# The sums of two layer norms: bf16 copies and bf16 squares replaced by float32 operands

## The chip, the cores and the metric

The kernel runs on all 8 cores of one Trainium2 chip. The metric is the device time in microseconds of the slowest core. The median of 3 runs is 2408.73 us (2408.63 to 2413.28).

## The reference

One transformer layer, with a layer norm behind each of its two parts, over x of shape (2, 4096, 2048) in float32:

```python
x = layernorm(x + attention(x, Wq, Wk, Wv, Wo))   # 16 query heads, 4 KV heads, window 512
x = layernorm(x + ffn(x, ...))                    # silu(x Wg') * (x Wu'), then Wd'; 2048 -> 8192 -> 2048
# layernorm: (x - mean) / sqrt(var + 1e-5) over the last axis (2048), with no scale and no bias
# Wg, Wu, Wd are integers 0..255: (w - 128) * a scale for each output row
```

## The kernel before

Each core computes 1024 tokens (and reads 512 more for the keys and values of its window). Activations lie transposed: the 2048 features are 16 blocks (KC = 16) of 128 partitions, the tokens lie along the free axis. The residual stream is S_sb, float32, 128 x (16 x 1024). All else that is large lies in one bf16 tile, ab, cut by offsets (abv(offset, n)).

The stages follow one another: projections for v, q and k; attention; the output projection psW (L465), whose results VectorE adds to S_sb (L474); the first layer norm; the feed-forward in two halves of 32 blocks (gate psG L685, up psU L693, then the sums of h psH L751 for the zero point, then the down projection psD, which starts each output with two float32 matmuls of one row, L791, and goes on with L795), whose results VectorE adds to S_sb (L805); the second layer norm; the output. Instructions are written engine by engine, and semaphores (tm for TensorE, vv for VectorE, ss for ScalarE, and others for DMA) order them. barrier() makes every engine wait for all counts so far; there is one before and one at the end of each norm. The first weights of the feed-forward are requested by GpSimd after the first norm's barrier.

emit_ln writes a layer norm. The features lie on partitions, so a sum over them is a matmul with a column of ones: out is 1 x 512. Its steps, with their lines:

1. ScalarE copies S_sb to bf16, 16 copies of 128 x 1024 (L499, to abv(rbf_o)).
2. First sum: for each half of the tokens (tt) 16 matmuls over k, ones_cb (bf16) against the copies, into psS1 (L511). Those of tt = 0 wait each for their copy.
3. ScalarE squares S_sb, 32 pieces of 128 x 512, to one of two bf16 buffers (L527); each waits until the matmul two before has read its buffer.
4. Second sum: 32 matmuls of the ones against the squares, into psS2 (L537), each of which waits for its square. Two float32 matmuls of 1 x 1 against 1 x 512 add eps (L542).
5. Mean, variance, reciprocal and root on one partition, by VectorE and ScalarE in turn (L551 to L580), then four float32 matmuls (L586 to L589) which spread both rows over 128 partitions.
6. VectorE multiplies and subtracts, 16 instructions each (L600, L605). In the first norm ScalarE writes the bf16 copy y1 of the result (L612).

Both norms call it with the copies' place free for them: y1_o in the first, h_o in the second. sq_sb is a float32 tile of 128 x 1024, in use in the feed-forward (L720 writes it) and for the mean in the norm. onc_sb is a float32 column of ones that is loaded at the start, and oncb_sb the bf16 one.

Of the kernel before, what the change touches and what calls it, by code (L numbers as in the profile page):

```python
# [19 lines left out]
KC = D // 128  # L20
# [8 lines left out]
def build_nc(debug=False, upto=99, dumps=None):  # L29
# [33 lines left out]
    with contextlib.ExitStack() as ctx:  # L63
        S_sb = ctx.enter_context(nc.sbuf_tensor("S_sb", [128, KC * T], F32))
        ab = ctx.enter_context(nc.sbuf_tensor("ab", [128, 65536], BF16))
        sq_sb = ctx.enter_context(nc.sbuf_tensor("sq_sb", [128, 1024], F32))
# [3 lines left out]
        onc_sb = ctx.enter_context(nc.sbuf_tensor("onc_sb", [128, 1], F32))  # L70
# [4 lines left out]
        oncb_sb = ctx.enter_context(nc.sbuf_tensor("oncb_sb", [128, 1], BF16))  # L75
        eps_sb = ctx.enter_context(nc.sbuf_tensor("eps_sb", [1, 512], F32))

        def abv(off, n):
            return ab[:, off:off + n]
# [9 lines left out]
        ss = ctx.enter_context(nc.semaphore("ss"))  # L89
# [7 lines left out]
        cnt = {k: 0 for k in sems}  # L97

        def inc(instr, name, step=1):
            cnt[name] += step  # L100
            instr.then_inc(sems[name], step)
            return cnt[name]
# [5 lines left out]
        block = ctx.enter_context(nc.Block())  # L108
# [377 lines left out]
        def emit_ln(write_bf16_to=None, rbf_o=None):  # L486
            _ln_id[0] += 1
            li = _ln_id[0]
            with nc.psum_tensor(f"psS1_{li}", [1, 1024], F32) as psS1, \
                 nc.psum_tensor(f"psS2_{li}", [1, 1024], F32) as psS2, \  # L490
                 nc.psum_tensor(f"psB1_{li}", [128, 1024], F32) as psB1, \
                 nc.psum_tensor(f"psB2_{li}", [128, 1024], F32) as psB2:
                ss0_rc = cnt["ss"]
                c_rc = [ss0_rc + k + 1 for k in range(KC)]

                @block.scalar
                def _(s):
                    for k in range(KC):
                        got = inc(s.copy(abv(rbf_o + 1024 * k, 1024),  # L499
                                         S_sb[:, 1024 * k:1024 * k + 1024]), "ss")  # L500
                        assert got == c_rc[k]

                @block.tensor
                def _(t):
                    t.wait_ge(sq, p0_sq)
                    last = None
                    for tt in range(2):
                        for k in range(KC):
                            if tt == 0:
                                t.wait_ge(ss, c_rc[k])  # L510
                            last = t.matmul(psS1[:1, 512 * tt:512 * tt + 512], oncb_sb[:, :1],  # L511
                                            abv(rbf_o + 1024 * k + 512 * tt, 512),
                                            start=(k == 0), stop=(k == KC - 1))
                    inc(last, "tm")
                tm0_sq = cnt["tm"]
                c_smm = [tm0_sq + j + 1 for j in range(2 * KC)]
                ss0_sq = cnt["ss"]
                c_sq = [ss0_sq + j + 1 for j in range(2 * KC)]

                @block.scalar  # L520
                def _(s):
                    for j in range(2 * KC):
                        tt, k = j // KC, j % KC
                        if j >= 2:
                            s.wait_ge(tm, c_smm[j - 2])
                        got = inc(
                            s.activation(abv(rbf_o + 16384 + 512 * (j % 2), 512),  # L527
                                         S_sb[:, 1024 * k + 512 * tt:1024 * k + 512 * tt + 512],
                                         AF.Square), "ss")
                        assert got == c_sq[j]  # L530

                @block.tensor
                def _(t):
                    for j in range(2 * KC):
                        tt, k = j // KC, j % KC
                        t.wait_ge(ss, c_sq[j])
                        got = t.matmul(psS2[:1, 512 * tt:512 * tt + 512], oncb_sb[:, :1],  # L537
                                       abv(rbf_o + 16384 + 512 * (j % 2), 512),
                                       start=(k == 0), stop=False)
                        assert inc(got, "tm") == c_smm[j]  # L540
                    for tt in range(2):
                        inc(t.matmul(psS2[:1, 512 * tt:512 * tt + 512], onr_sb[:1, :1],  # L542
                                     eps_sb[:1, :], start=False, stop=True), "tm")
                tm_sums = cnt["tm"]

                psM = sq_sb[0:1, 0:1024]
                psQ2 = st_sb[:1, 0:1024]
                @block.vector
                def _(v):
                    v.wait_ge(tm, tm_sums)  # L550
                    inc(v.tensor_scalar(psM, psS1[:1, :], 1.0 / D, None, ALU.mult), "vv")  # L551
                c1 = cnt["vv"]

                @block.scalar
                def _(s):
                    s.wait_ge(vv, c1)
                    inc(s.activation(psQ2, psM, AF.Square), "ss")
                c2 = cnt["ss"]

                @block.vector  # L560
                def _(v):
                    v.wait_ge(ss, c2)
                    inc(v.scalar_tensor_tensor(psS2[:1, :], psS2[:1, :], 1.0 / D,
                                               psQ2, ALU.mult, ALU.subtract), "vv")
                    v.wait_ge(vv, cnt["vv"])
                    inc(v.reciprocal(psS2[:1, :], psS2[:1, :]), "vv")
                c3 = cnt["vv"]

                @block.scalar
                def _(s):  # L570
                    s.wait_ge(vv, c3)
                    inc(s.activation(psS2[:1, :], psS2[:1, :], AF.Sqrt), "ss")
                c4 = cnt["ss"]

                @block.vector
                def _(v):
                    v.wait_ge(ss, c4)
                    inc(v.tensor_tensor(psQ2, psM, psS2[:1, :], ALU.mult), "vv")
                    v.wait_ge(vv, cnt["vv"])
                    inc(v.tensor_copy(psM, psS2[:1, :]), "vv")  # L580
                c5 = cnt["vv"]

                @block.tensor
                def _(t):
                    t.wait_ge(vv, c5)
                    t.matmul(psB1[:, 0:512], onr_sb[:1, :], sq_sb[0:1, 0:512], start=True, stop=True)  # L586
                    t.matmul(psB1[:, 512:1024], onr_sb[:1, :], sq_sb[0:1, 512:1024], start=True, stop=True)
                    t.matmul(psB2[:, 0:512], onr_sb[:1, :], st_sb[:1, 0:512], start=True, stop=True)
                    inc(t.matmul(psB2[:, 512:1024], onr_sb[:1, :], st_sb[:1, 512:1024],  # L589
                                 start=True, stop=True), "tm")  # L590
                tm_bc = cnt["tm"]

                ln_done = [None] * KC

                @block.vector
                def _(v, ln_done=ln_done):
                    v.wait_ge(tm, tm_bc)
                    for k in range(KC):
                        sl = S_sb[:, 1024 * k:1024 * k + 1024]
                        inc(v.tensor_tensor(sl, sl, psB1[:, :], ALU.mult), "vv")  # L600
                    mid = cnt["vv"]
                    v.wait_ge(vv, mid)
                    for k in range(KC):
                        sl = S_sb[:, 1024 * k:1024 * k + 1024]
                        ln_done[k] = inc(v.tensor_tensor(sl, sl, psB2[:, :], ALU.subtract), "vv")  # L605

                if write_bf16_to is not None:
                    @block.scalar
                    def _(s, ln_done=ln_done):
                        for k in range(KC):  # L610
                            s.wait_ge(vv, ln_done[k])
                            inc(s.copy(abv(write_bf16_to + 1024 * k, 1024),  # L612
                                       S_sb[:, 1024 * k:1024 * k + 1024]), "ss")

                barrier()
                return ln_done

        emit_ln(write_bf16_to=y1_o, rbf_o=y1_o)

        if debug and "y1" in dumps:  # L620
# [198 lines left out]
        if debug and "r2" in dumps:  # L819
# [4 lines left out]
            barrier()  # L824

        ln2_done = emit_ln(write_bf16_to=None, rbf_o=h_o)

        @block.sync
# [93 lines left out]
```

## Time and profile before

| what | us |
|---|---|
| median of 3 runs | 2408.73 |
| the profiled execution: its time | 2411.91 |
| its span on the slowest core (core 4) | 2410.3 |
| spans of the 8 cores | 2394.1 to 2410.3 |
| first norm, from the table load to the end of y1 | 711.14 to 820.61 |
| second norm, its first record | 2277.82 |

The profile is that of core 4, and every time of the rows below is counted from the start of its span. PE is TensorE's matmuls, PEld its weight loads, DVE is VectorE, ACT ScalarE, POOL GpSimd. The granted clock of TensorE is given as a share of 2.4 GHz: 1.00 is 2.4, 0.50 is 1.2 GHz. TensorE is busy 83% of the span, VectorE 20%, ScalarE 15%, and the mean granted clock is 0.901.

### The profile page before, as it was taken

The page shows a single profiled execution, that of the slowest core. Times are in us where ns is not written, and L with a number is a line of the kernel's source. Part 1 is how long each engine was busy: PE and PEld are TensorE (multiplying, and loading weights), DVE is VectorE, ACT ScalarE, POOL GpSimd, SP SyncE. Part 2 cuts the span into 40 slices and gives each one's busy share as a digit, 9 for nine tenths or more (in the row PEclk, how much of TensorE's full clock was granted, in tenths as well). Part 3 has the DMA queues.
Part 4 walks back from the last instruction along what each step waited for, and adds up shares of the span by engine and source line. Part 5 has one row for each costly group of instructions (what it writes and reads, how often), then busy time and mean ns, then how long its engine had stood idle before and what let it go on. Part 6 is the DMA issues. An engine that isn't in the chain of part 4 may idle for free.

```text
span 2410.3 us, 23828 instructions; the slowest of 8 cores (2394.1 to 2410.3 us)
## 1 busy us (share of the span) xinstructions
PE 2012.4 (83%) x9317; PEld 916.8 (38%) x9496; DVE 471.0 (20%) x800; ACT 367.0 (15%) x640; POOL 129.0 (5%) x248
## 2 busy tenths in 40 slices
PE   0789766666985299999999999999999999999850
PEld 0334344444431144444443444444444443444310
DVE  0111266665111510010010000010010010000025
ACT  0000055555014301001010000001001010000140
POOL 4000000000000000000000000000000000000000
PEclk9999966666995599999999999999999999999955
DMA  9444200000430354344333333344344330333103
GB/s 218 62 92 70 53 1 1 1 1 1 70 53 0 53 89 87 70 75 83 70 71 53 70 64 58 67 74 87 70 75 83 70 71 18 70 65 58 35 0 139
DMA packets 38419, 147.68 MB, mean 61 GB/s; under 512 B 4643, under 2 KB 8869, under 8 KB 33958
## 3 DMA queue, kind: packets, MB, share of 16 engines
q0 software_dynamic: 35136, 127.94, 30.2%
q1 hardware_dynamic: 3174, 18.20, 2.3%
q8 instruction: 79, 1.29, 0.2%
q14 instruction: 30, 0.25, 0.0%
HBM read 265.66 MB, written 8.39 MB: 114 GB/s over the span
## 4 chain that ended last, share of the span: by engine, by line
PE 78%; DVE 7%; issue 4%; ACT 4%; another core or an unknown queue 3%; DMA 2%; DVEq 0%; ACTq 0%; POOL 0%; POOLq 0%
PE psD L795 19%; PE psG L685 18%; PE psU L693 18%; PE psW L465 5%; PE psQ L218 5%; PE psD L791 3%; PE pT L345 3%; PE pv L358 2%; DVE S_sb L600 2%; DVE S_sb L605 1%; PE psH L751 1%; ACT ab L499 1%; PE psQ L227 1%; DVE Dm_sb L386 1%
## 5 line engine op out<-in xcount | busy, mean ns | idle before, releaser
L685 PE MATMUL psG<-ab 128*128 128x512 bf16 x2006 | 451.5, 380 | 51.4 <-DMA ab<-wu_is 47.2
L795 PE MATMUL psD<-ab 128*128 128x512 bf16 x2004 | 449.9, 381 | 4.8 <-issue 3.7
L693 PE MATMUL psU<-ab 128*128 128x512 bf16 x2008 | 450.0, 379 | 2.1
L685 PEld LDWEIGHTS psG<-ab 128*128 128x128 bf16 x2048 | 200.7, 98 | 293.8 <-issue 54.1
L795 PEld LDWEIGHTS psD<-ab 128*128 128x128 bf16 x2048 | 195.8, 98 | 277.7 <-issue 52.9
L693 PEld LDWEIGHTS psU<-ab 128*128 128x128 bf16 x2048 | 200.2, 98 | 241.8
L705 DVE SCALAR_TENSOR_TENSOR ab<-psU,scl_sb,sq_sb 128x512 bf16<-128x512 f32 x128 | 90.2, 746 | 810.3 <-PE psU L693 810.3
L720 ACT ACTIVATE sq_sb<-psG,scl_sb 128x512 f32<-128x512 f32 x128 | 87.9, 687 | 775.1 <-PE psG L685 775.1
L345 PE MATMUL pT<-Dm_sb,ab 128*128 128x128 bf16 x640 | 77.4, 274 | 100.5 <-DVE Dm_sb L386 60.3
L805 DVE SCALAR_TENSOR_TENSOR S_sb<-psD,scl_sb,S_sb 128x1024 f32<-128x1024 f32 x32 | 41.1, 1283 | 481.5 <-PE psD L795 481.5
L218 PE MATMUL psQ<-ab 128*128 128x512 bf16 x501 | 111.6, 383 | 12.6 <-DMA ab<-wq_os 11.9
L465 PE MATMUL psW<-ab 128*128 128x512 bf16 x502 | 112.4, 385 | 1.3 <-DVE ab L378 0.8
L345 PEld LDWEIGHTS pT<-Dm_sb,ab 128*128 128x128 bf16 x640 | 50.9, 119 | 161.7 <-issue 161.7
L400 ACT ACTIVATE ab<-sc 128x640 bf16<-128x640 f32 x128 | 90.0, 703 | 118.3 <-DVE sc L372 107.6
L372 DVE TENSOR_TENSOR sc<-sc,ab 128x640 f32<-128x640 f32 x128 | 105.5, 825 | 1.8 <-PE sc L336 0.9
L407 ACT CAST ab<-pT 128x640 bf16<-128x640 f32 x128 | 87.5, 684 | 2.8 <-PE pT L345 2.8
L183 PE MATMUL psA<-ab 128*128 128x512 bf16 x95 | 23.9, 407 | 74.5 <-DMA ab<-x_all 74.5
L358 PE MATMUL pv<-ab 128*128 128x128 bf16 x640 | 84.8, 289 | 0.5 <-DVE ab L378 0.5
L106 POOL DMA_DIRECT2D ab<-wg_is x64 | 33.8, 527 | 915.6 <-PE psU L693 726.2
L218 PEld LDWEIGHTS psQ<-ab 128*128 128x128 bf16 x512 | 50.4, 99 | 73.8 <-issue 14.6
L465 PEld LDWEIGHTS psW<-ab 128*128 128x128 bf16 x512 | 50.5, 99 | 63.0 <-issue 4.1
L791 PE MATMUL psD<-st_sb,nr_sb 1*128 1x512 f32 x128 | 71.9, 641 | 2.9 <-DVE st_sb L760 2.9
(74 smaller groups left out, 935.7 us busy)
## 6 DMA issues: line engine op xcount, KB each, us to landing
ab<-wg_is POOLq DMA_DIRECT2D x64, 512.0 KB, 5.0
ab<-wu_is POOLq DMA_DIRECT2D x64, 512.0 KB, 7.0
ab<-wd_os POOLq DMA_DIRECT2D x32, 1024.0 KB, 8.0
ab<-wq_os POOLq DMA_DIRECT2D x16, 512.0 KB, 5.0
ab<-wo_os POOLq DMA_DIRECT2D x16, 512.0 KB, 5.0
y<-S_sb SPq DMA_DIRECT2D x16, 512.0 KB, 6.7
ab<-x_all POOLq DMA_DIRECT2D x16, 256.0 KB, 45.6
ab<-wv_ks POOLq DMA_DIRECT2D x16, 128.0 KB, 32.1
```

Of the source, the lines that this page charges most:

```text
L218: last = t.matmul(ps[:, 512 * tt:512 * tt + 512], abv(wbuf_o + 2048 * (o % 2) + 128 * k, 128), abv(rhs_base + k * rhs_stride + rhs_off + 5 ...
L345: last = t.matmul(pTp[:, 128 * b:128 * b + 128], abv(probs_o + 640 * (m % 3) + 128 * b, 128), Dm_sb[:, 128 * (m % 3):128 * (m % 3) + 128], ...
L358: last = t.matmul(pvs[m % 2][:, :], abv(vT_o + 512 * (mqt + b) + 128 * (mh // 4), 128), abv(pT_o + 640 * (m % 2) + 128 * b, 128), start=(b ...
L372: assert inc(v.tensor_tensor(scs[n % 2][:, :], scs[n % 2][:, :], abv(mask_o + 640 * qt, 640), ALU.add), "vv") == c_msk[n]
L400: s.activation(abv(probs_o + 640 * (n % 3), 640), scs[n % 2][:, :], AF.Exp, bias=0.0, scale=1.0 / 128.0, accum_out=sums_sb[:, 2 * (n % 3): ...
L465: last = t.matmul(psQ[o % 2][:, 512 * tt:512 * tt + 512], abv(wbuf_o + 2048 * (o % 2) + 128 * k, 128), abv(attn_o + 1024 * k + 512 * tt, 512),
L685: last = t.matmul(psG[i % 2][:, 512 * tt:512 * tt + 512], abv(wgu_o + 4096 * (i % 2) + 128 * k, 128), abv(y1_o + 1024 * k + 512 * tt, 512) ...
L693: last = t.matmul(psU[i % 2][:, 512 * tt:512 * tt + 512], abv(wgu_o + 4096 * (i % 2) + 2048 + 128 * k, 128), abv(y1_o + 1024 * k + 512 * t ...
L705: v.scalar_tensor_tensor(abv(h_o + 1024 * i + 512 * tt, 512), psU[i % 2][:, 512 * tt:512 * tt + 512], scl_sb[:, 64 + ii:64 + ii + 1], sq_s ...
L720: s.activation(sq_sb[:, 512 * tt:512 * tt + 512], psG[i % 2][:, 512 * tt:512 * tt + 512], AF.Silu, bias=0.0, scale=scl_sb[:, ii:ii + 1]), ...
L791: t.matmul(psD[o % 2][:, 512 * tt:512 * tt + 512], nr_sb[:1, :], st_sb[:1, 512 * tt:512 * tt + 512], start=True, stop=False)
L795: last = t.matmul(psD[o % 2][:, 512 * tt:512 * tt + 512], abv(wd_o + 4096 * (o % 2) + 128 * i, 128), abv(h_o + 1024 * i + 512 * tt, 512), ...
```

## The change

In emit_ln the 16 copies to bf16 go, with the waits for them. The matmuls of the first sum read S_sb itself, in float32, with the float32 ones. The squares are written as float32 to the two halves of sq_sb, and the matmuls of the second sum read these with the float32 ones. Counts, order and buffering of the squares and of all that follows stay. The function is called twice.

```diff
-                ss0_rc = cnt["ss"]
-                c_rc = [ss0_rc + k + 1 for k in range(KC)]
-
-                @block.scalar
-                def _(s):
-                    for k in range(KC):
-                        got = inc(s.copy(abv(rbf_o + 1024 * k, 1024),
-                                         S_sb[:, 1024 * k:1024 * k + 1024]), "ss")
-                        assert got == c_rc[k]
-
                 @block.tensor
                 def _(t):
                     t.wait_ge(sq, p0_sq)
                     last = None
                     for tt in range(2):
                         for k in range(KC):
-                            if tt == 0:
-                                t.wait_ge(ss, c_rc[k])
-                            last = t.matmul(psS1[:1, 512 * tt:512 * tt + 512], oncb_sb[:, :1],
-                                            abv(rbf_o + 1024 * k + 512 * tt, 512),
+                            last = t.matmul(psS1[:1, 512 * tt:512 * tt + 512], onc_sb[:, :1],
+                                            S_sb[:, 1024 * k + 512 * tt:1024 * k + 512 * tt + 512],
                                             start=(k == 0), stop=(k == KC - 1))
                     inc(last, "tm")
...
                         got = inc(
-                            s.activation(abv(rbf_o + 16384 + 512 * (j % 2), 512),
+                            s.activation(sq_sb[:, 512 * (j % 2):512 * (j % 2) + 512],
                                          S_sb[:, 1024 * k + 512 * tt:1024 * k + 512 * tt + 512],
                                          AF.Square), "ss")
...
                         t.wait_ge(ss, c_sq[j])
-                        got = t.matmul(psS2[:1, 512 * tt:512 * tt + 512], oncb_sb[:, :1],
-                                       abv(rbf_o + 16384 + 512 * (j % 2), 512),
+                        got = t.matmul(psS2[:1, 512 * tt:512 * tt + 512], onc_sb[:, :1],
+                                       sq_sb[:, 512 * (j % 2):512 * (j % 2) + 512],
                                        start=(k == 0), stop=False)
```

## Rows read from the trace of the kernel before

**Rows 1.** Busy time by stretch, two stretches of the first norm's sums, with the columns' names.

```profile
core 4: us, PE busy (x) PEld busy (x) DVE busy (x) ACT busy (x) POOL busy (x), PEclk, DMA share, GB/s
...
711.00:729.00 18.00, 9.71 (x18) 1.55 (x19) 0.00 (x0) 17.82 (x19) 0.00 (x0) 0.58 0.00 0
729.00:757.00 28.00, 21.70 (x50) 4.07 (x49) 0.00 (x0) 18.36 (x32) 0.00 (x0) 0.62 0.00 0
```

**Rows 2.** The timeline of the first norm: start, length, engine, line, instruction [idle before].

```profile
709.62 1.22 DVE L474 TENSOR_TENSOR S_sb<-S_sb,psW 128x1024 f32<-128x1024 f32 x1 [5.69 <-PE psW L465]
711.14 1.28 ACT L499 ACT_TABLE_LOAD   x1 [116.30 <-DVE S_sb L474]
712.43 15.24 ACT L499 CAST ab<-S_sb 128x1024 bf16<-128x1024 f32 x16
...
713.62 0.38 PE L511 MATMUL psS<-ab,oncb_sb 128*1 128x512 bf16 x1 [4.11 <-ACT ab L499]
...
715.51 0.58 PE L511 MATMUL psS<-ab,oncb_sb 128*1 128x512 bf16 x1 [0.36 <-ACT ab L499]
...
727.82 5.36 PE L511 MATMUL psS<-ab,oncb_sb 128*1 128x512 bf16 x17 [0.36 <-ACT ab L499]
...
755.32 3.56 PE L542 MATMUL psS<-eps_sb,onr_sb 1*1 1x512 f32 x4
```

**Rows 3.** The chain that ended last, at both ends of the second norm's sums.

```profile
2276.35 1.29 DVE S_sb L805
...
2277.82 1.28 ACT L499
...
2321.79 3.51 PE psS L542 x4
```

**Rows 4.** The same chain: the sums of h, and one square with its matmuls.

```profile
1276.26 15.67 PE psH L751 x64
...
2314.88 0.60 PE psS L537
...
2315.56 0.64 ACT ab L527
2316.20 0.14 issue
```

**Rows 5.** Groups of instructions: shapes and count, busy us and mean ns, idle before.

```profile
L720 ACT ACTIVATE sq_sb<-psG,scl_sb 128x512 f32<-128x512 f32 x128 | 87.9, 687 | 775.1 <-PE psG L685 775.1
L791 PE MATMUL psD<-st_sb,nr_sb 1*128 1x512 f32 x128 | 71.9, 641 | 2.9 <-DVE st_sb L760 2.9
L527 ACT ACTIVATE ab<-S_sb 128x512 bf16<-128x512 f32 x64 | 36.8, 621 | 14.3 <-PE psS L537 13.7
```

**Rows 6.** The timeline of TensorE in the first norm's broadcast.

```profile
777.58 1.91 PE L587 MATMUL psB<-sq_sb,onr_sb 1*128 1x512 f32 x2
779.29 1.91 PE L588 MATMUL psB<-st_sb,onr_sb 1*128 1x512 f32 x2
```

**Rows 7.** The timeline of TensorE around one float32 call in the down projection.

```profile
1327.25 0.69 PE L791 MATMUL psD<-st_sb,nr_sb 1*128 1x512 f32 x1
...
1327.78 0.59 PE L791 MATMUL psD<-st_sb,nr_sb 1*128 1x512 f32 x1
...
1328.30 0.39 PE L795 MATMUL psD<-ab 128*128 128x512 bf16 x1
```

**Rows 8.** Busy time by stretch: the end of the broadcast, and the sums of h.

```profile
779.00:783.00 4.00, 3.90 (x5) 1.00 (x3) 0.00 (x0) 0.00 (x0) 0.00 (x0) 0.50 0.00 0
783.00:790.00 7.00, 0.00 (x0) 0.00 (x0) 6.99 (x7) 0.00 (x0) 0.00 (x0) 0.50 0.00 0
1276.00:1280.00 4.00, 3.74 (x11) 1.24 (x12) 0.00 (x0) 0.00 (x0) 1.05 (x2) 0.63 0.52 83
1280.00:1284.00 4.00, 4.00 (x19) 1.49 (x18) 0.00 (x0) 0.00 (x0) 0.53 (x1) 0.94 0.99 183
1284.00:1288.00 4.00, 4.00 (x20) 1.58 (x19) 0.00 (x0) 0.00 (x0) 0.53 (x1) 1.00 1.02 144
```

## The prediction

> **What bounds the kernel now.** I read the busy time by stretch first. TensorE is nearly full in the projections and the feed-forward, and what lies outside is the attention and the two layer norms. In the sums of the first norm it has work for 9.71 of 18 us and then 21.70 of 28 us, at a mean clock of 0.58 and 0.62, with no transfer in flight [rows 1]. Every other engine waits for the norm (the next weights are asked for only after it), so a microsecond in a norm is one in the span.
>
> The timeline gives the lengths [rows 2]. The last residual add ends at 710.84 (709.62 + 1.22). ScalarE loads its table at 711.14, then makes 16 bf16 copies in 15.24 us (0.953 each). The matmuls of the first half of the first sum follow the copies one by one, so the other half (x17, from 727.82) runs when the last copy is there. Then come 32 Square instructions and 32 matmuls in turn, until the eps matmuls start at 755.32. From 711.14 to 755.32 it is 44.2 us. In the second norm the add ends at 2277.64, and the eps matmuls stand at 2321.79: 43.9 us from the table load at 2277.82 [rows 3]. I take 44.0 us for each.
>
> The chain of waits gives the pace of the squares [rows 4]: a matmul ends and 0.08 us later Square runs 0.64 us, then 0.14 us to the next matmul of 0.60 us. That makes 1.46 us for two, since there are two buffers: 0.73 us a matmul and 23 us for 32. This loop waits for latency; neither engine is full.
>
> **The change, part by part.** Twice in the kernel, once for each norm:
>
> (a) The 16 copies go. They and their table load take 16.5 us of each 44.0 us. Nothing else reads the copies: L612 writes y1 anew from S_sb after the norm. The first sum no longer waits for ScalarE. It starts at the barrier (about 711.1) with all 32 matmuls back to back, while ScalarE does its table load and the first two squares under it and then waits for the first matmul of the second sum. So the sums become nearly pure TensorE time.
>
> (b) All 64 ones-matmuls become float32, 128 rows, one weight column. No such form is in the trace; the nearest are the float32 matmuls with one row. Each of them appears as two records (x128 of L791 for 64 calls [rows 5]). At clock 0.50 calls start at 777.58 and 779.29 [rows 6]: 1.71 us each, so four times 512 columns at 1.2 GHz (4 x 0.427). At full clock, L791's records start at 1327.25 and 1327.78 and the next bf16 matmul at 1328.30 [rows 7]: 1.05 us for a call. Four times 512 columns at 2.4 GHz would be 0.853 us, which leaves 0.1 us more for each record, perhaps its 128-column weight load. With one weight column that excess may vanish, so the bounds at full clock are 0.853 and 1.05 us. I take 1.05, the row itself.
>
> The Trainium skill (FP8 and Floating Point Precision, TensorE Precision Notes) has true FP32 as four passes. The 1.71 us agree with that; its reduced-precision FP32, a single read of truncated data, would give a call the bf16 price and turn the sign, and is the last rival's way. No run here shows such a call.
>
> (c) Squares are written as float32 to sq_sb. L527 takes 621 ns with bf16 output; L720, which reads PSUM and a scale and writes float32, takes 687 ns [rows 5]. The bounds are 0.62 and 0.69 us. The cover is the matmul between: two matmuls take 2.10 us, and the loop of one (matmul 1.12 with its drain, 0.08, 0.64, 0.14) takes 1.98 us. So the squares are hidden, with 0.1 us to spare at 1.05 us a call and 1.4 us at 1.71. At 0.853 the cover is gone: the loop is then about 1.85 us for two, 0.93 a matmul, and the second sum takes 29.6 and not 27.3 us.
>
> (d) sq_sb has no reader during the sums; the mean goes into it only after them. No DMA moves and no queue is passed. Everything from L551 on keeps its length, and the weight requests of the feed-forward shift whole with the norm.
>
> **Which clock.** This is the large unknown: 1.05 or 1.71 us a call. The clock is full when the projection ends. Today it is down for most of the sums (mean 0.58): TensorE has nothing for 4.11 us ahead of them and then waits 0.36 us in every 0.95 [rows 1, 2]. After the change there is only the 1.5 us gap of the barrier and then a solid stream. For a solid stream of one-column bf16 matmuls the rows show recovery: in the sums of h (L751, x64 from 1276.26 [rows 4]) the clock is 0.63 just after a gap, 0.94 in the next 4 us and 1.00 after that [rows 8]. One weight column is thus no hindrance. For float32 the only solid stream is the broadcast (L586 to L589, four calls of 1.71 us), 6.8 us, and the clock is still 0.50 in its last 4 us and after it [rows 6, 8]. That stream has one row, the new one 128. Either the one row or the float32 keeps the clock down there; no row separates them. One row in 128 moves hardly any data, while the new matmuls feed all rows as L751's do, and I give that reading somewhat more.
>
> The Trainium skill (TensorE: Matmul & The Clock Gate, Part 1) has TensorE go to 2.4 GHz on sustained matmul work and names no exception for float32. By that rule the sums run at 1.05 us a call; the broadcast does not follow the rule as it stands.
>
> **The sum, at full clock.** 64 calls x 1.05 = 67.2 us against 44.0: +23.2 us. The two eps calls follow while the clock is still up: four records of 0.53 = 2.1 us in place of 3.51 [rows 3]: -1.4. That is +21.8 for a norm and +43.6 for both. The profiled execution took 2411.9 us (span 2410.3), so 2455.5; the median of the runs is 3.2 us lower than it, and the same shift gives 2452.3. At 0.853 a call: 27.3 + 29.6 = 56.9 us, +12.9 - 1.4 = +11.5 a norm, +23 in all, 2432. A dip of the clock over two calls in each norm would add 1.3 us each. This case's own range is 2431 to 2456.
>
> **The rivals.**
>
> *Half clock throughout.* Float32 as such does not hold the clock: it falls soon after the start and stays at 0.50, as in the broadcast. Then 64 x 1.71 = 109.2 us, less up to 2.3 us (three or four calls that still start at full clock): 106.9 to 109.2 against 44.0, +63 to +65 a norm, +126 to +130 in all: 2535 to 2539. For it: the only float32 stream in the trace [rows 8]. Against it: that stream has one row.
>
> *Mixed.* The first sum holds the clock, but in the second the small waits for the squares let it drop: 33.6 + 54.6 = 88.2 us, +44.2 a norm, 2497. For it: the clock falls today while TensorE is busy 21.70 of 28 us [rows 1]. Against it: at 1.05 us a call the squares leave no gap.
>
> *Not slower.* A one-column float32 call costs far less than a one-row one, as if it were one pass of 0.216 us. Then the first sum takes 6.9 us, the second goes at the pace of ScalarE's loop (0.62 to 0.73 a matmul, 20 to 23 us), and the removed copies are a net gain: 27 to 30 us against 44.0, twice, 2375 to 2381. It decides from 44.0 / 64 = 0.69 us a call downwards. Against it: every float32 record in the trace shows at least 0.52 us, two a call, with one weight column too (L542: four records in 3.51 us at half clock) [rows 3, 7].
>
> That the change does nothing to the path is excluded: the sums are on the chain and no other work is there to cover them [rows 1, 4].
>
> **How the numbers follow.** Full clock 0.52, half clock 0.41, mixed 0.04, not slower 0.03. The predicted time is that of the likeliest, 2452 us. To leave out no more than 2 in 10 the range must take in the half-clock case: 2430 to 2540; the likeliest case alone has 2431 to 2456. 0.2% is 4.8 us, about what a measurement of this kernel can tell from no change. Slower by more than that has 0.97, within it 0.01, faster 0.02.
>
> **What would show it.** No copies on L499's place, and ScalarE's only work before the second sum two squares under the first. The first sum starts within 0.5 us of the last residual add. Two records a call, 128 in all for each norm. Full clock: starts of calls 0.85 to 1.05 us apart and a granted clock near 1.00 from the first call to the eps calls; 57 to 67 us from barrier to eps calls. Half clock: 1.71 us apart, 0.50, 107 to 109 us. Squares are hidden if their idle time is ended by the matmul each time and TensorE has none in the second sum. The stretch from L551 to the end of the norm should be as long as before. The prediction is wrong if the clock in that stream is the other one, or if a one-column float32 call has a price outside 0.85 to 1.05 us at full clock; a sum that depends on one unseen form could fail in both ways.

## The result and the profile after

The changed kernel takes 1.0107 of the time before (95% interval 1.0092 to 1.0121): the medians are 2437.4 us over 8 runs and 2412.3 us over 10, so it is about 25 us slower. In some executions the cores of one die show a lower granted clock and take longer; the ratios here leave those out. Forecast were 2452 us and slower with a chance of 0.97; the range was 2430 to 2540.

The groups of the sums in the changed kernel (shapes and count, busy us and mean ns, idle before). L499 is the first sum, L515 the squares, L525 the second sum, L530 the eps calls:

```profile
L525 PE MATMUL psS<-sq_sb,onc_sb 128*1 128x512 f32 x128 | 60.1, 590 | 0.4
L499 PE MATMUL psS<-S_sb,onc_sb 128*1 128x512 f32 x128 | 56.9, 607 | 4.0 <-DVE S_sb L474 2.1 <-DVE S_sb L793 1.9
L515 ACT ACTIVATE sq_sb<-S_sb 128x512 f32<-128x512 f32 x64 | 40.1, 630 | 72.9 <-PE psS L525 72.8
L530 PE MATMUL psS<-eps_sb,onr_sb 1*1 1x512 f32 x8 | 3.7, 586 | 0.0
```

There are two records a call, 128 records for each norm. TensorE has only 0.4 us of idle time in the second sum of both norms, and ScalarE's idle time is ended by the matmuls. The squares with float32 output take 630 ns (621 with bf16 output [rows 5]).

The chain of waits of the changed kernel in the second norm:

```profile
2289.28 1.29 DVE S_sb L793
2290.58 0.49 issue
2291.06 27.63 PE psS L499 x64
...
2320.42 1.88 PE psS L525 x4
2322.31 1.88 PE psS L525 x4
```

The first sum is 27.63 us, so 0.86 us a call. The second goes on at 1.89 us for each two calls (x4 is four records), 0.94 each. From the last residual add (2290.57) to the eps calls it is 58.1 us; before, it was 44.1 us (2277.64 to 2321.79) [rows 3]. From the mean to the last subtraction it is 60.5 us in both kernels, as forecast.

Busy time by stretch around the start of the first norm's sums, slowest core of the changed kernel (the columns are those of [rows 1]), then the second norm's:

```profile
715.00:719.00 4.00, 3.89 (x6) 0.66 (x7) 0.00 (x0) 2.06 (x3) 0.00 (x0) 0.66 0.00 0
719.00:723.00 4.00, 4.00 (x10) 0.80 (x9) 0.00 (x0) 0.00 (x0) 0.00 (x0) 0.91 0.00 0
723.00:727.00 4.00, 4.00 (x10) 0.76 (x9) 0.00 (x0) 0.00 (x0) 0.00 (x0) 1.00 0.00 0
...
2294.00:2318.00 24.00, 24.00 (x57) 4.70 (x56) 0.00 (x0) 0.00 (x0) 0.00 (x0) 1.00 0.00 0
2318.00:2348.00 30.00, 29.82 (x65) 3.74 (x64) 0.00 (x0) 18.91 (x30) 0.00 (x0) 1.00 0.00 0
```

A float32 stream of 128 rows holds the full clock for 55 us, and it brings it back: here the clock falls about 1 us into the stream, and 4 us of float32 calls later it is on its way up again (0.66, 0.91, 1.00). The two sums of a norm, from their first start to that of the eps calls, take 57.6 us where the clock did not dip and 59.3 us on the four cores where it did (0, 1, 3 and 7, in the first norm). TensorE was idle for 2.1 us ahead of the sums on cores 0 and 7 and just as long on cores 2, 4, 5 and 6, which did not dip, so the length of that gap alone does not decide it. Before the change the sums ran mostly at half clock, with means of 0.58 and 0.62 [rows 1].

### The profile page after: what moved, and what is told of

The parts are those of the page before. It is cut to its first block, busy times and chain, and to the rows that moved or that the text cites. A ratio compares the mean times of both kernels' runs of the same rounds, so it can differ in the third digit from the quotient of the medians.

```text
span 2435.6 us, 24197 instructions; the slowest of 8 cores (2427.9 to 2435.6 us)
## 1 busy us (share of the span) xinstructions
PE 2078.8 (85%) x9624; PEld 923.2 (38%) x9624; DVE 471.1 (19%) x800; ACT 337.6 (14%) x606; POOL 129.0 (5%) x248
## 4 chain that ended last, share of the span: by engine, by line
PE 82%; DVE 7%; issue 4%; another core or an unknown queue 3%; ACT 2%; DMA 1%; DVEq 0%; ACTq 0%; POOL 0%; POOLq 0%
PE psD L783 18%; PE psG L673 18%; PE psU L681 18%; PE psW L465 5%; PE psQ L218 5%; PE psD L779 3%; PE pT L345 3%; PE psS L525 2%; PE psS L499 2%; PE pv L358 2%; DVE S_sb L588 1%; DVE S_sb L593 1%; PE psQ L227 1%; PE psH L739 1%
## 5 line engine op out<-in xcount | busy, mean ns | idle before, releaser
L335 PE MATMUL sc<-ab 128*128 128x512 bf16 x128 | 71.9, 562 | 4.8 <-ACT ab L400 2.7
```

## The experiments

Times are medians, ratios are to the kernel before, with 95% intervals. Sums of a norm are from the first record of the first sum to the first eps record.

**e1: only the first sum in float32.** In the kernel before:

```diff
-    (the 16 copies of L499 and the waits for them)
-    t.matmul(psS1[...], oncb_sb[:, :1], abv(rbf_o + 1024 * k + 512 * tt, 512), ...)
+    t.matmul(psS1[...], onc_sb[:, :1], S_sb[:, 1024 * k + 512 * tt:1024 * k + 512 * tt + 512], ...)
```

> The kernel before, with only the first sum changed: no copies, 32 float32 calls on S_sb; squares and second sum stay bf16. My account (a float32 call with 128 rows costs 0.857 us at full clock and holds it): first sum 27.5 us behind the barrier, second sum at the old pace of 0.6 to 0.73 us a matmul, 50 us from barrier to eps calls against 44.0, so +6 us a norm and about +12 us in all (2421 to 2425 against 2409 to 2412). Rival, that the first sum gains by the removed copies and all the loss is in the squares: the time of before or less, and the second sum alone carries +26 us.

Measured: 2422.9 us, 1.0049 (1.0031 to 1.0067).

**e2: only squares and second sum in float32**, the rest as before:

```diff
-    s.activation(abv(rbf_o + 16384 + 512 * (j % 2), 512), S_sb[...], AF.Square)
+    s.activation(sq_sb[:, 512 * (j % 2):512 * (j % 2) + 512], S_sb[...], AF.Square)
-    t.matmul(psS2[...], oncb_sb[:, :1], abv(rbf_o + 16384 + 512 * (j % 2), 512), ...)
+    t.matmul(psS2[...], onc_sb[:, :1], sq_sb[:, 512 * (j % 2):512 * (j % 2) + 512], ...)
```

> The kernel before, with only squares and second sum in float32; the copies and the bf16 first sum stay. My account: 21.9 us up to the first matmul of the second sum as before, then 32 x 0.945 = 30.2 us, less 1.4 us for eps calls at full clock: +6.7 us a norm, +13 us in all. With the other half alone (+12) this adds up to the +26 of the whole change. Rival, that the copies' absence is a gain and the second sum carries the whole loss: +26 us or more here. Second rival, that the clock falls at the start of the squares, as it does before: 32 x 1.71 = 54.7 us, +31 us a norm, +62 in all.

Measured: 2425.7 us, 1.0055 (1.0037 to 1.0074). The halves cost +12 and +13 us, as expected, and add up to 1.0104, against 1.0107 for the whole. The copies that go in e1 are worth less than the price of 32 float32 calls. The chain of waits of e1 in the second norm:

```profile
2284.10 27.63 PE psS L499 x64
2312.04 0.64 ACT ab L515
2313.29 0.64 ACT ab L515
...
2333.03 3.51 PE psS L530 x4
```

The first sum is 27.63 us, in place of 21.9 from the copies' table load to the end of the bf16 one. The bf16 squares start at a pace of 1.25 us for two, while the clock is up, and later go at 1.46; the eps calls then run at half clock (3.51 us). In e2 the chain shows the same 1.88 us for two calls as in the full change, and the clock does not fall at the start of the squares: the second rival of e2 is out.

**e3: four float32 square buffers** in the changed kernel (in the part of ab that the copies had):

```diff
-    if j >= 2: s.wait_ge(tm, c_smm[j - 2])
+    if j >= 4: s.wait_ge(tm, c_smm[j - 4])
-    sq_sb[:, 512 * (j % 2):512 * (j % 2) + 512]                                   # square's output, matmul's input
+    ab[:, rbf_o + 1024 * (j % 4):rbf_o + 1024 * (j % 4) + 1024].bitcast(F32)
```

> The changed kernel with four float32 buffers for the squares and not two. My account: in the second sum two calls take 1.89 us and not 2 x 0.857 because each buffer comes back only after matmul, semaphore, square and semaphore; with four buffers TensorE should run solid at 0.857 us a call, the second sum takes 27.5 and not 30.2 us, -2.7 us a norm and -5 us in all against the changed kernel (about +20 us over before). Rival, that a call is itself slower while ScalarE writes the squares beside it: no change, +26 us over before.

Measured: 2430.8 us, 1.0088 (1.0071 to 1.0105), about 5 us less than the changed kernel; the intervals of the two ratios overlap, so the chain has to decide:

```profile
2288.99 27.63 PE psS L499 x64
2316.61 27.47 PE psS L525 x64
2344.08 1.82 PE psS L530 x4
```

The second sum is 27.47 us, solid, where it was 30.1. So 2.6 us a norm was the wait for a buffer, and a call costs 0.86 us with ScalarE writing beside it, which puts the rival out.

**e6: 128 weight columns in the first sum** of the changed kernel:

```diff
+    on2_sb = sbuf_tensor([128, 128], F32); memset(on2_sb, 1.0); psS1 has 128 rows
-    t.matmul(psS1[:1, 512 * tt:512 * tt + 512], onc_sb[:, :1], ...)
+    t.matmul(psS1[:, 512 * tt:512 * tt + 512], on2_sb[:, :], ...)
```

> The changed kernel with 128 float32 columns of ones as weights in the first sum and not one (psS1 has 128 rows, of which the first is read, so the result is the same). If the 0.1 us more for each record that L791 showed is its 128-column weight load: 1.05 us a call, first sum 33.7 us and not 27.5, +6 us a norm and +12 us over the changed kernel. If it was the single row of L791's data, or its place between bf16 matmuls: 0.857 us a call and no change.

Measured: 2438.5 us in a single run. Its first sum in the chain of waits, and its weight loads in the groups:

```profile
2292.11 27.70 PE psS L504 x64
```

```profile
L504 PEld LDWEIGHTS psS<-S_sb,on_sb 128*128 128x128 f32 x128 | 24.2, 190 | 34.6 <-issue 34.6
```

27.70 against 27.63 us: inside the stream a weight load of 190 ns instead of 85 is hidden under the call before it. So the prediction's guess for the 0.1 us of L791, its 128-column weight load, does not hold for calls that follow their own kind; e9 comes back to it.

**e9: the zero-point calls grouped**, in the kernel before:

```diff
     for tt in range(2):
         t.matmul(psD[...], nr_sb[:1, :], st_sb[...], start=True, stop=False)
+    for tt in range(2):
         for i in range(32):
             last = t.matmul(psD[...], abv(wd_o + ...), abv(h_o + ...), start=False, stop=(i == 31))
```

> The kernel before, with the two float32 zero-point calls of each down-projection output set one behind the other ahead of its 64 bf16 matmuls, and not each ahead of its 32. It asks where the 0.1 us more per record of L791 comes from, since 128 weight columns alone do not cost it. If it is the change between bf16 and float32 (into and out of each call), only the outer records pay: four records in about 1.9 us and not 2.1, and 3 to 9 us less over 32 outputs. If it belongs to every float32 record of one row with 128 weight columns: 0.52 us a record as before, and no change in all.

Measured: 2405.5 us, 0.9977 (0.9964 to 0.9991). TensorE's timeline at one output, core 6 of e9 (each line is from a narrow window, so a record can stand in two lines):

```profile
1354.61 0.38 PE L796 MATMUL psD<-ab 128*128 128x512 bf16 x1
...
1354.92 0.69 PE L791 MATMUL psD<-st_sb,nr_sb 1*128 1x512 f32 x1
...
1355.45 1.02 PE L791 MATMUL psD<-st_sb,nr_sb 1*128 1x512 f32 x2
...
1355.88 1.02 PE L791 MATMUL psD<-st_sb,nr_sb 1*128 1x512 f32 x2
1356.31 0.59 PE L791 MATMUL psD<-st_sb,nr_sb 1*128 1x512 f32 x1
1356.83 0.39 PE L796 MATMUL psD<-ab 128*128 128x512 bf16 x1
```

Starts are 0.31 us apart into float32 (0.216 among bf16 matmuls), then 0.53, 0.43, 0.43, and 0.52 out of it. The two inner records cost 0.43 us, with one row and 128 weight columns. The excess sits at the ends, about 0.1 us at each of three places, 0.29 us for each stay among the bf16 matmuls. e9 has 32 stays fewer, 9 us by that. On cores where the clock stays full, a down projection takes 252.9 us from its first start to its last against 257.7 before, so 9.5 us less for both. The time shows 5.5 us less (2 to 9); where the rest went is not shown.

The type is not what costs, though. At an end of L791 the type changes, but the number of rows does too (128 and 1). Other runs change one thing at a time: e2 and e8 the type alone, e6 the weight columns alone, the changed kernel the rows alone (with the one column as it was), and stand below in this order, two lines each (cores 0, 2, 1 and 7).

```profile
2289.20 0.38 PE L511 MATMUL psS<-ab,oncb_sb 128*1 128x512 bf16 x1
2289.42 0.59 PE L537 MATMUL psS<-sq_sb,onc_sb 128*1 128x512 f32 x1
...
2292.19 0.59 PE L499 MATMUL psS<-S_sb,onc_sb 128*1 128x512 f32 x1
2292.62 0.38 PE L523 MATMUL psS<-ab,oncb_sb 128*1 128x512 bf16 x1
...
2319.22 0.59 PE L504 MATMUL psS<-S_sb,on_sb 128*128 128x512 f32 x1
2319.74 0.59 PE L530 MATMUL psS<-sq_sb,onc_sb 128*1 128x512 f32 x1
...
2348.16 0.59 PE L525 MATMUL psS<-sq_sb,onc_sb 128*1 128x512 f32 x1
2348.68 0.58 PE L530 MATMUL psS<-eps_sb,onr_sb 1*1 1x512 f32 x1
```

With the same shape on both sides the change of type costs nothing: 0.22 us behind a bf16 matmul and 0.43 behind a float32 record, as inside either stream. With float32 on both sides, a change from 128 weight columns to one, or from 128 rows to one, puts the next start at 0.52 us and not at 0.43. This holds in both norms on all eight cores. The second record's 0.53 goes with the 128 weight columns: the eps calls of e10, which have 128, show 0.53 between their first two starts behind bf16 matmuls, and those of e8, which have one, 0.43. So the weight load that the prediction suspected does show in the first record behind a change of shape.

**e4: one row in the first sum** of the changed kernel. Its first sum covers one feature of 128 in each block in the first norm (float32), and in the second norm it is 128 bf16 matmuls of one row that are no sum of x at all:

```diff
-    t.matmul(psS1[...], onc_sb[:, :1], S_sb[:, 1024 * k + 512 * tt:...], ...)
+    t.matmul(psS1[...], onc_sb[:1, :1], S_sb[:1, 1024 * k + 512 * tt:...], ...)       # first norm
+    t.matmul(psS1[...], oncb_sb[:1, :1], ab[:1, rbf_o + 1024 * k:...], ...)           # second norm, 128 calls
```

> The changed kernel with a first sum over one row of 128 (127 of 128 features are left out of the mean): in the first norm 32 float32 calls as before, in the second norm 128 bf16 matmuls of one row on whatever lies in the tile (its first sum is no sum at all). It asks what kept the clock at 0.50 in the broadcast. If one row does it, whatever the type: the clock falls in both streams and the first norm's sum takes 52 to 55 us (32 x 1.71), the second's 52 to 55 us (128 x 0.427), some +50 us over the changed kernel. If only float32 of one row does it: 52 to 55 us in the first norm and 27.5 us (128 x 0.214) in the second, about +25 us. If neither (it was the short stream or its cold start): 27.5 us in both.

Measured: 2486.2 us in the profiled execution (spans of 2472.8 to 2484.6 us), some 49 us over the changed kernel. Core 1 of e4, first norm and second norm:

```profile
720.00:760.00 40.00, 40.00 (x48) 5.60 (x47) 0.00 (x0) 0.00 (x0) 0.00 (x0) 0.50 0.00 0
...
764.00:768.00 4.00, 3.99 (x8) 0.48 (x6) 0.00 (x0) 2.20 (x4) 0.00 (x0) 0.77 0.00 0
768.00:790.00 22.00, 21.88 (x48) 2.62 (x46) 0.00 (x0) 14.60 (x24) 0.00 (x0) 1.00 0.01 1
```

```profile
2320.00:2360.00 40.00, 40.00 (x95) 11.48 (x94) 0.00 (x0) 0.00 (x0) 0.00 (x0) 0.50 0.00 0
```

TensorE is busy 40 of 40 us in both and the clock is 0.50, with float32 and with bf16. When the 128-row calls of the second sum begin (761.85 in the first norm), it is up within some 5 us. Both sums of a norm take 83.1 to 86.4 us in place of 57.6. So the row decides, not the type: the rival of a special float32 case is out, and so is that of a stream that was only too short.

**e5: 32 rows in the first norm, 64 in the second**, 32 float32 calls in each norm, with `[:32]` and `[:64]` in place of e4's `[:1]` (the first sum leaves out three quarters and one half of the features):

> The changed kernel with a first sum over 32 rows in the first norm and 64 rows in the second, both float32 (three quarters and one half of the features are left out of the mean). If the clock follows how many rows of data go in, 32 rows should lose it (52 to 55 us) and 64 rows may or may not (27.5 or 52 to 55 us). If only a single row is special: 27.5 us in both. The price of a call at a given clock should not depend on rows in any account.

Measured: 2485.6 us in a single run. With 32 rows all eight cores lose the clock (sums of 84.6 to 86.3 us). With 64 rows the cores of one execution part: 57.7 us on cores 0, 3, 4 and 7, and 84.6 to 84.7 us on cores 1, 2, 5 and 6. Two of them in the second norm, core 0 and then core 1, each with the start of the stream and the idle time ahead of it:

```profile
2308.45 11.74 PE L506 MATMUL psS<-S_sb,onc_sb 64*1 64x512 f32 x27 [1.89 <-DVE S_sb L800]
...
2312.00:2316.00 4.00, 4.00 (x11) 0.73 (x9) 0.00 (x0) 0.00 (x0) 0.00 (x0) 1.00 0.00 0
...
2320.00:2330.00 10.00, 10.00 (x25) 1.94 (x24) 0.00 (x0) 0.00 (x0) 0.00 (x0) 1.00 0.00 0
```

```profile
2313.34 7.41 PE L506 MATMUL psS<-S_sb,onc_sb 64*1 64x512 f32 x11 [1.89 <-DVE S_sb L800]
...
2312.00:2316.00 4.00, 2.66 (x6) 0.51 (x7) 0.84 (x1) 2.43 (x3) 0.00 (x0) 0.94 0.02 4
2316.00:2320.00 4.00, 4.00 (x6) 0.62 (x5) 0.00 (x0) 0.00 (x0) 0.00 (x0) 0.50 0.00 0
...
2345.00:2360.00 15.00, 15.00 (x19) 2.25 (x18) 0.00 (x0) 0.00 (x0) 0.00 (x0) 0.50 0.00 0
```

On four cores the clock stays up under 64 rows; on the other four it falls about 2 us into the stream, and 64 rows do not lift it again. The gap ahead of the stream is 1.89 us on both of these cores, and 1.86 on core 3, which kept the clock, as on core 2, which lost it. So its length does not part them, and what does stays open.

**e8: float32 first sum, bf16 squares with a place each** (32 places behind rbf_o + 16384, no wait for a buffer), from e1:

```diff
-    if j >= 2: s.wait_ge(tm, c_smm[j - 2])
-    abv(rbf_o + 16384 + 512 * (j % 2), 512)
+    abv(rbf_o + 16384 + 512 * j, 512)
```

> The float32 first sum without copies, with bf16 squares that each have a place of their own, so that ScalarE runs ahead under the first sum. My account: 27.5 us for the first sum, then 32 x 0.216 = 6.9 us, 35 us against 44.0, less 1.4 us for eps calls at full clock: -10 us a norm, about 2388 to 2392 us in all. This is the part of the change that pays (a sum that waits for no copy) with the float32 price paid once. Rival, that squares and float32 reads of the same tile slow each other: first sum longer than 28 us.

Measured: 2385.7 us, 0.9906 (0.9882 to 0.993). The chain of waits in its second norm:

```profile
2265.15 27.63 PE psS L499 x64
2292.78 6.91 PE psS L523 x32
```

34.5 us for both sums, and 22 us less in all, a little more than the expected 2388 to 2392 us allowed. The first sum keeps its 27.63 us with ScalarE squaring the same tile beside it, so the rival is out.

**e7: bf16, copies on VectorE** beside squares on ScalarE, from the kernel before:

```diff
-    ScalarE: 16 copies, then 32 squares of 128 x 512 in two buffers
+    VectorE: v.tensor_copy(abv(rbf_o + 1024 * k, 1024), S_sb[:, 1024 * k:...])                    # 16
+    ScalarE: s.activation(abv(rbf_o + 16384 + 1024 * k, 1024), S_sb[:, 1024 * k:...], AF.Square)  # 16, no buffer wait
+    TensorE: for each k: wait for copy k, 2 matmuls to psS1; wait for square k, 2 matmuls to psS2
```

> A bf16 version: VectorE, idle in the sums, makes the 16 bf16 copies while ScalarE squares 16 pieces of 128 x 1024 to bf16, each with a place of its own, and TensorE takes both sums block by block behind them. The sums then end with the slower of the two engines: ScalarE 1.28 + 15.25 us, VectorE 16 x 1.21 = 19.4 us at most. 17.5 to 20.5 us from barrier to eps calls against 44.0: -24 to -28 us a norm, 2353 to 2363 us in all. Against it: if both engines slow each other at the same data, or if the matmuls at half clock (1.71 us for four a block) become the limit, 28 us and 2378 us.

Measured: 2352.6 us, 0.9761 (0.9719 to 0.9803). A second set, e11, is the same kernel:

> The version with copies on VectorE once more, beside the others on one chip: 2350 to 2355 us, 0.976 of before.

Measured: 2351.7 us, 0.9756 (0.9734 to 0.9778). The copies take 0.69 us each on VectorE, not 1.21, and both sums 16.7 to 18.3 us from their first start to that of the eps calls.

**e10: the sums on all partitions**, from e7, with a bf16 tile of ones of 128 x 128:

```diff
-    t.matmul(psS1[:1, ...], oncb_sb[:, :1], ...)      # psS2 likewise, eps with onr_sb[:1, :1]
+    t.matmul(psS1[:, ...], on2_sb[:, :], ...)         # psS2 likewise, eps with onr_sb[:1, :]
     (mean, variance, reciprocal, root on [:, 0:1024] and not on [:1, 0:1024])
-    4 broadcast matmuls to psB1 and psB2, and the copy of L580
```

> The version with copies on VectorE, and ones of 128 x 128 (bf16) as weights, so that both sums arrive on all 128 partitions and the four float32 broadcast matmuls and one copy go. By the price found for 128 weight columns (none), the sums keep their length, and 7.4 us (broadcast, from the last row operation to the first multiply) plus 1.3 us (copy) go from each norm: -17 us against the version with copies on VectorE, about 2335 us. Against it: if 128 columns of output slow the sums, they take longer than 17 us; if VectorE and ScalarE work on 128 partitions at another pace than on one, the steps between change.

Measured: 2334.5 us, 0.9699 (0.965 to 0.9748). The timeline of core 3 in the first norm, from the eps calls to the first multiply:

```profile
721.55 1.98 PE L531 MATMUL psS<-eps_sb,onr_sb 1*128 1x512 f32 x4
723.64 1.22 DVE L540 TENSOR_SCALAR sq_sb<-psS 128x1024 f32<-128x1024 f32 x1 [10.21 <-PE psS L531]
...
728.73 6.57 DVE L555 RECIPROCAL psS<-psS 128x1024 f32<-128x1024 f32 x1
...
737.78 1.22 DVE L567 TENSOR_TENSOR sq_sb<-sq_sb,psS 128x1024 f32<-128x1024 f32 x1 [2.48 <-ACT psS L561]
739.11 18.18 DVE L577 TENSOR_TENSOR S_sb<-S_sb,psS 128x1024 f32<-128x1024 f32 x16
```

An operation on 128 partitions takes about what it took on one (reciprocal 6.57 us, 6.55 before), and the multiply starts 0.1 us behind the last row operation. The sums take 16.5 to 18.1 us, as in e7, and the time is 17 us below e11's, as expected.

## Why the prediction was right, and where its size was off

**Direction and mechanism** held. The norm is on the chain alone; the copies' 16.5 us went, a call became float32 at the price of four bf16 ones (0.86 against 0.216), and the clock stayed full but for the dip at the entry. The forecast gave full clock 0.52 and half clock 0.41, so this was close to an even choice, and the wide range that held the measured time near its lower end came from the half-clock case. e4 and e5 show what the trace before could not: the single row of the broadcast kept the clock down, not float32. The reading that had "somewhat more" was the right one.

The Trainium skill (TensorE: Matmul & The Clock Gate, Part 1) has TensorE at 2.4 GHz under sustained matmul work. By that rule the sums ran as they did, and the 128-row streams agree with it (1.00 for 55 us). The 40 us streams of one row at 0.50 do not.

**Step (b), the price of a call at full clock,** is the term that was mis-sized: 1.05 us taken, 0.86 measured. Both bounds were named, and I took the row, for the reason that it was a row. But L791's call stands alone between bf16 matmuls of 128 rows, and the new calls stand in a stream of their own shape. e9 shows 0.43 us for a record with its own kind on both sides. Of the 0.2 us that L791 has over that, half is the 128 weight columns in the first record behind a change of shape, as the prediction guessed, and half the change of shape behind the second; the type has no part in it (e2, e6, e8, e10). The neighbours of the instruction were the difference that mattered.

**Step (c), the squares,** held as written for the low price: at 0.853 us a call "the loop is then about 1.85 us for two", and it is 1.89. With four buffers the 2.6 us a norm came back (e3). The matmuls' idle time does not show this loss (0.4 us): a record has 0.59 us in the profile and the next starts 0.43 us behind it, or 0.61 where a buffer is waited for, so the wait leaves hardly a gap. Only the starts show it. One more reading of step (c) was wrong, with nothing resting on it: "1.4 us at 1.71" leaves the matmul in the loop at its full-clock length; with the 1.91 us that the profile has for two records at half clock [rows 6] the loop is 2.77 us and the spare 0.65.

**The sum by the measured terms** for one norm on core 4 of both profiles, from the residual add to the mean: 60.4 and 60.1 us against 48.2 and 47.8, so +12.3 each and +24.5 together, plus 1.7 us on a core whose clock dips at the entry: 26.2. Measured were 1.07% of 2412, 25.8. The prediction's low case had +23. It lacks 0.7 us in the sums of each norm (57.6 us and not 56.9), and the start, which was put at about 0.3 us behind the add and is 0.47 to 0.87; it took 0.3 us too little off for the eps calls; and it left out the dip, which it named and put at 1.3. TensorE's gap ahead of the sums was put at 1.5 us and is 1.9 and 2.1.

**The other rivals.** Half clock did not happen with 128 rows (e4 shows what it would have cost: 27 us more for one of the two sums, in each norm). Mixed did not happen: the waits of the second sum, 0.18 us in each 1.89, left the clock at 1.00. Not slower failed at the price: the break-even was 0.69 us a call and the call costs 0.86.

## What to carry to other kernels

A float32 matmul costs four bf16 ones, and one column of ones does not make it cheaper. To save a copy by it pays only if the copy holds up more than that; first see whether an idle engine can make the copy (e7) and whether the buffers let the producer run ahead (e3, e8). When a price is taken from a row, look at what stands before and behind that instruction: here its neighbours were of another shape, and the price so taken made up 19 us of a forecast of 44 (67.2 in place of 57.6 us, twice).

## What the runs showed of the hardware that I had not expected

- The granted clock follows the rows of data that go in. Solid streams of 1 row (float32 and bf16) and of 32 rows stayed at 0.50 for 40 us and more, 64 rows held 1.00 on four cores and sat at 0.50 on four others in one execution, with the same gap ahead, and 128 rows with one weight column brought it back.
- A matmul of another shape than the one before it starts about 0.09 us late, whether the rows or the weight columns change (0.52 in place of 0.43 us, 0.31 in place of 0.216). A change between bf16 and float32 at the same shape costs nothing (0.216 and 0.43).
- In a stream 128 weight columns cost no more than one, in float32 (27.70 against 27.63 us for 32 calls) and in bf16 (e10). Only the first float32 record behind another shape takes 0.1 us more with 128 (0.53 against 0.43), so a sum can arrive on all partitions for next to nothing.
- VectorE casts 128 x 1024 from float32 to bf16 in 0.69 us, when ScalarE takes 1.04.
